# Border rows scaled whole and zeroed again, and TensorE's program written out, in a kernel of a deformable and a binarised convolution

## The reference, cut to what matters

```python
def _dcnv4(x, dw_w, dw_b, om_w, om_b, vp_w, vp_b, op_w):
    xdw = conv3x3_depthwise(x, dw_w, padding='SAME') + dw_b    # zero outside the image
    om = (xdw @ om_w + om_b).reshape(n, h, w, G, KK * 3)       # per group and tap: dx, dy, mask
    value = (x @ vp_w + vp_b).reshape(n, h, w, G, GC)
    # bilinear samples of value at (pixel + tap + offset), times mask, summed over the 9 taps
    return out @ op_w

x = x + _dcnv4(_gn(x), ...)
x = x + binarised_conv(_gn(x), ...)
```

## Time and profile before

| | us |
|---|---|
| median of 3 runs | 4247.4 (4243.7 to 4248.2) |
| the profiled execution | 4246.0 |
| its span, first to last instruction | 4244.2 |
| TensorE busy | 3872.8 (91%) |
| VectorE busy | 3561.1 (84%) |
| ScalarE busy | 2423.4 (57%) |
| GpSimd busy | 569.8 (13%) |
| mean granted TensorE clock | 0.973 |

### The profile page before, as it was taken

One profiled execution on the slowest core, in us unless ns is written; L12 is line 12 of the kernel. 1 busy time (PEld: TensorE's weight loads), 2 busy tenths in 40 slices (PEclk: granted clock), 3 DMA queues, 4 the chain that ended last, 5 costly groups with the idle time before them and its releaser, 6 DMA issues. The chain is left out here.

```text
span 4244.2 us, 94584 instructions
## 1 busy us (share of the span) xinstructions
PE 3872.8 (91%) x38382; PEld 2480.9 (58%) x38382; DVE 3561.1 (84%) x2896; ACT 2423.4 (57%) x5027; POOL 569.8 (13%) x480
## 2 busy tenths in 40 slices
PE   3899999999999999999999999999999985888988
PEld 1466666666666666666666666666666663333333
DVE  2799899989998899899989998999899993556554
ACT  4666666666666666666666666666666622333332
POOL 0011111111111111111111111111111110222222
PEclk9999999999999999999999999999999996999999
DMA  4454455445544554555445544554454433222321
GB/s 129 108 115 100 101 126 123 99 103 119 120 100 104 120 119 99 109 123 119 99 101 125 124 99 101 121 129 99 100 106 104 79 57 133 89 90 90 136 92 60
DMA packets 308092, 453.20 MB, mean 107 GB/s; under 512 B 33456, under 2 KB 239024, under 8 KB 301872
## 3 DMA queue, kind: packets, MB, share of 16 engines
q0 software_dynamic: 95168, 197.15, 25.9%
q1 hardware_dynamic: 212464, 249.71, 19.4%
HBM read 245.38 MB, written 67.11 MB: 74 GB/s over the span
## 5 line engine op out<-in xcount | busy, mean ns | idle before, releaser
L982 DVE TENSOR_TENSOR pv<-val,wsum 128x2048 f32<-128x2048 f32 x800 | 1810.3, 2283 | 11.1 <-PE ps_add L791 11.0
L791 PEld LDWEIGHTS ps_add<-ident,pv 128*128 128x128 f32 x12800 | 1399.7, 142 | 325.7 <-issue 220.7
L791 PE MATMUL ps_add<-ident,pv 128*128 128x128 f32 x12800 | 1525.0, 275 | 39.5 <-DVE pv L982 31.0
L746 PE MATMUL ps_om<-xdw,omw 128*32 128x256 f32 x13824 | 884.4, 389 | 124.7 <-ACT hat L579 109.1
L746 PEld LDWEIGHTS ps_om<-xdw,omw 128*32 128x32 f32 x13824 | 395.0, 111 | 431.7 <-ACT hat L579 120.8
L470 POOL DMA_DIRECT2D wsum<-prod x192 | 226.0, 1255 | 2688.6 <-DVE wsum L935 2688.6
L577 ACT ACTIVATE hat<-ps_om,omb 128x256 f32<-128x256 f32 x576 | 275.4, 478 | 537.0 <-PE ps_om L746 537.0
L935 DVE TENSOR_TENSOR prod<-hat,mwy 128x1536 f32<-128x1536 f32 (+1 forms) x384 | 525.2, 1395 | 59.0 <-DMA wsum<-prod 42.5
L1530 PE MATMUL ps_c<-c_sgn,c_ksgn 128*128 128x512 bf16 x2304 | 518.7, 384 | 2.5 <-DVE c_res L1647 2.5
L542 ACT ACTIVATE tri<-tri,gn_tri 96x512 f32<-96x512 f32 (+3 forms) x812 | 473.5, 647 | 6.0 <-DMA tri<-in_zeros_dram 0.5
L921 DVE TENSOR_TENSOR mwy<-hat,msk 128x768 f32<-128x768 f32 x288 | 274.1, 952 | 223.7 <-ACT hat L591 223.5
(11 more groups left out here) (102 smaller groups left out, 2791.2 us busy)
## 6 DMA issues: line engine op xcount, KB each, us to landing
wsum<-prod POOLq DMA_DIRECT2D x160, 768.0 KB, 6.9
tri<-in_x_dram SPq DMA_DIRECT2D x725, 128.0 KB, 2.9
win<-in_x_dram SPq DMA_DIRECT2D x144, 256.0 KB, 3.3
xres<-in_x_dram POOLq DMA_DIRECT2D x128, 256.0 KB, 9.0
x<-xres SPq DMA_DIRECT2D x128, 256.0 KB, 4.1
c_x<-x SPq DMA_DIRECT2D x8, 4096.0 KB, 13.0
out_dram<-c_x SPq DMA_DIRECT2D x32, 1024.0 KB, 4.0
acc<-in_x_dram POOLq DMA_DIRECT2D x14, 1024.0 KB, 5.6
```

The lines of the kernel that those rows point to most:

```text
L746: mm = nc.tensor.matmul(ps_om[G * q:G * q + G, (par + i) % 2, 0:TOK], omw[:, h, comp, :], xdw[:, j % 2, h, q, :], start=h == 0, stop=h == ...
L791: mm = nc.tensor.matmul(ps_add[:, tb, c, :], pv[:, (j + uv) % PBUF, c, P * tb:P * tb + P], consts["ident"][:, :], start=uv == 0 and c % 4 ...
L982: nc.vector.tensor_tensor(pv[:, (j + uv) % PBUF, :, :].rearrange("p c (r w) -> p c r w", w=W), val[:, :, SR * j + u:SR * j + u + SR, v:v + ...
```

## The change

Two edits. First, `normalise_tri` takes a tuple of `qp` and scales whole pieces; where both `qp` are normalised in one place, a piece covers both (96x1024). At an image's border the row outside is scaled along and then set to zero again by one `Copy` with scale 0, which waits on a new semaphore for the scaling to be done. `tri_normed` is raised by the number of `qp`, at the end. Second, TensorE's program of layer 0 calls `step` for all 32 steps with plain numbers, so its loop and its register arithmetic are gone. The other engines keep their loops.

```diff
-                def normalise_tri(n, j, h, qp):
-                    ...
-                    parts = [(0, KROWS, 2 * qp, 2 * qp + 2, 0, SR)]
-                    if j == 0 and qp == 0:
-                        parts = [(0, KROWS, 0, 1, 1, SR), (32, 64, 0, 1, 0, 1), (64, KROWS, 0, 1, 0, 1),
-                                 (0, KROWS, 1, 2, 0, SR)]
-                    elif j == STEPS - 1 and qp == 1:
-                        parts = [(0, KROWS, Q - 2, Q - 1, 0, SR), (0, KROWS, Q - 1, Q, 0, SR - 1),
-                                 (0, 64, Q - 1, Q, SR - 1, SR)]
+                def normalise_tri(n, j, h, qps):
+                    for qp in qps:
+                        ...
                     for c in range(CB):
-                        for p0, p1, q0, q1, r0, r1 in parts:
-                            v = tri_of(n, j, h)[p0:p1, c, q0:q1, r0:r1, :]
-                            last = nc.scalar.activation(v, v, ACT.Identity, bias=gn_tri[p0:p1, j % 2, 2 * c + 1, h:h + 1],
-                                                        scale=gn_tri[p0:p1, j % 2, 2 * c, h:h + 1])
-                    last.then_inc(tri_normed, 1)
+                        v = tri_of(n, j, h)[0:KROWS, c, 2 * qps[0]:2 * qps[-1] + 2, :, :]
+                        last = nc.scalar.activation(v, v, ACT.Identity, bias=gn_tri[0:KROWS, j % 2, 2 * c + 1, h:h + 1],
+                                                    scale=gn_tri[0:KROWS, j % 2, 2 * c, h:h + 1])
+                    outside = None
+                    if j == 0 and 0 in qps:
+                        outside = tri_of(n, j, h)[0:32, :, 0, 0, :]
+                    elif j == STEPS - 1 and 1 in qps:
+                        outside = tri_of(n, j, h)[64:KROWS, :, Q - 1, SR - 1, :]
+                    if outside is not None:
+                        last.then_inc(tri_scaled, 1)
+                        act.wait_ge(tri_scaled, 2 * CH * n + (0 if j == 0 else CH) + h + 1)
+                        last = nc.scalar.activation(outside, outside, ACT.Copy, scale=0.0)
+                    last.then_inc(tri_normed, len(qps))
...
-                for qp in range(2):
-                    normalise_tri(0, 0, 1, qp)
+                normalise_tri(0, 0, 1, (0, 1))
...
                         if k in DW_AT[1:3] and not last:
-                            normalise_tri(n1, j1, 1, DW_AT.index(k) - 1)
+                            normalise_tri(n1, j1, 1, (DW_AT.index(k) - 1,))
...
-                            for qp in range(2):
-                                normalise_tri(n2, j2, 0, qp)
+                            normalise_tri(n2, j2, 0, (0, 1))
...
-                steps_of_images(pe, step)
+                for n in range(NI):
+                    for j in range(STEPS):
+                        step(n, j, (n, j) == (0, 0), (n, j) == (NI - 1, STEPS - 1))
```

More of the change, by code:

```diff
@@ L284, in layer0 @@
         tri_loaded, tri_normed = [sem("tri_loaded0"), sem("tri_loaded1")], sem("tri_normed")
-        gn_spread = sem("gn_spread")
+        gn_spread, tri_scaled = sem("gn_spread"), sem("tri_scaled")
         bg_full, bg_free = sem("bg_full"), sem("bg_free")
@@ L524, in normalise @@
                     last.then_inc(win_normed, 1)
-                def normalise_tri(n, j, h, qp):
[L527 to L530, removed]
-                    parts = [(0, KROWS, 2 * qp, 2 * qp + 2, 0, SR)]
-                    if j == 0 and qp == 0:
-                        parts = [(0, KROWS, 0, 1, 1, SR), (32, 64, 0, 1, 0, 1), (64, KROWS, 0, 1, 0, 1),
-                                 (0, KROWS, 1, 2, 0, SR)]
-                    elif j == STEPS - 1 and qp == 1:
-                        parts = [(0, KROWS, Q - 2, Q - 1, 0, SR), (0, KROWS, Q - 1, Q, 0, SR - 1),
-                                 (0, 64, Q - 1, Q, SR - 1, SR)]
-                    for c in range(CB):
-                        for p0, p1, q0, q1, r0, r1 in parts:
-                            v = tri_of(n, j, h)[p0:p1, c, q0:q1, r0:r1, :]
-                            last = nc.scalar.activation(v, v, ACT.Identity, bias=gn_tri[p0:p1, j % 2, 2 * c + 1, h:h + 1],
-                                                        scale=gn_tri[p0:p1, j % 2, 2 * c, h:h + 1])
-                    last.then_inc(tri_normed, 1)
@@ new lines, in normalise_tri @@
+                def normalise_tri(n, j, h, qps):
+                    for qp in qps:
+                        if tri_of(n, j, h) is tri_first:
+                            act.wait_ge(tri_first_loaded[qp], 16 * tri_loads(j, qp))
+                        else:
+                            act.wait_ge(tri_loaded[qp], 16 * (tri_loads_before(n, j, h, qp) + tri_loads(j, qp)))
+                    for c in range(CB):
+                        v = tri_of(n, j, h)[0:KROWS, c, 2 * qps[0]:2 * qps[-1] + 2, :, :]
[11 more added lines that the diff above has]
+                    last.then_inc(tri_normed, len(qps))
@@ L626, in _ @@
                 act.wait_ge(val_zero, 6)
-                for qp in range(2):
-                    normalise_tri(0, 0, 0, qp)
+                normalise_tri(0, 0, 0, (0, 1))
                 act.wait_ge(weights_loaded, WL)
@@ L643, in _ @@
                 hats(0, 0, 1)
-                for qp in range(2):
-                    normalise_tri(0, 1, 0, qp)
+                normalise_tri(0, 1, 0, (0, 1))
                 def step(n, j, first, last):
```

## The result

| | before | after |
|---|---|---|
| median of the runs, us | 4246.3 (4243.7 to 4248.2, 4 runs) | 4146.5 (4144.0 to 4147.6, 4 runs) |
| span of the profiled execution | 4244.2 | 4143.6 |
| TensorE / VectorE busy | 3872.8 / 3561.1 | 3848.2 / 3560.1 |
| ScalarE busy | 2423.4 | 2288.7 |
| mean granted TensorE clock | 0.973 | 0.982 |

The ratio is 0.9765 (95% interval 0.9748 to 0.9782): 99.8 us less. The forecast was 4144 in a range of 4130 to 4180. Of all executions of this and the following kernels one, of d1_cut_in_j2_j3, was slow (5029.8 us at a granted clock of 0.746) and is left out of that kernel's median.

What follows compares the result with a forecast made beforehand. TensorE, held up by ScalarE's hats, was taken to bound j=0 and j=3, VectorE j=1 and j=2. Terms 66.5 + 2.8 + 4.3 + 6.9 + 22 = 102.5 us gave 4144 us, range 4130 to 4180 with the first two rivals.

Steps and rivals of the forecast that it cites:

- Start of j=3: Last step of seven images: shorter border-form scaling cuts TensorE's stalls for hats, 9.5 us an image, 66.5 us in all.
- the three parts: In j=3, per image: 5.3 us off the first stall, 2.3 from full clock behind it, 2.3 for the second stall.
- The 0.4 given away to VectorE: In j=3, 9.5 us an image was taken instead of 9.9, as VectorE is late next.
- Rival 1: VectorE takes over in j=3, so only 34 us come back instead of 66.5, giving 4176 us; chance 0.14.
- Before the loop: Start-up: the second border form's wait of 7.14 us shrinks by 5.3 and the matmuls behind it by 1.6, 6.9 us.
- j=0, plain form and closings: Starts of j=0: plain form's 0.62 us wait goes, 4.3 us; TensorE's loop removed at five closings, 22 us.
- Rival 2: Another engine's backward branch takes the place of TensorE's, so the 22 us do not come: 4166 us; chance 0.09.
- j=1 and j=2: Gain costed at zero in seven images, where VectorE is unbroken; 2.8 us taken in the last image.
- The pieces' own time: On ScalarE, the merged border form falls from 10.74 to 5.4 us, the unmerged one in j=3 from 7.91 to 3.4.
- rival 4: 96x1024 costs twice the 512 piece with no fixed part saved: 11 us less gain, 4155 us; chance 0.05.
- rival 3: TensorE's written-out program stalls for instruction fetch once in each step, 106 us, making it slower at 4271 us; chance 0.03.

Runs made afterwards that it cites:

- d1_cut_in_j2_j3: Changed kernel with the old cut pieces put back for steps j=2 and j=3 only: 4150.4 us, median of three runs.
- d2: Changed kernel with the old cut pieces put back for the second half of j=0, images after the first: 4162.0 us.
- f1: Changed kernel with VectorE's statistics reading 64 of every 512 columns, so its result is another one: 4090.7 us.
- e1: Changed kernel with TensorE's loop kept, so only the change to normalise_tri: 4161.4 us.
- e2: Kernel before with only TensorE's program written out, normalise_tri as before: 4230.5 us.
- e3: Changed kernel with pieces scaled whole but each qp for itself, eight of 96x512 instead of four of 96x1024: 4170.2 us.
- e5: Changed kernel with the loops of ScalarE, VectorE and SyncE written out too: 4145.2 us.
- h1: Changed kernel with SyncE's stores of a step's result moved behind the second twelve loads: 4138.2 us.
- after_again: The changed kernel itself, word for word, run again on the same chip as the two kernels with SyncE's order changed: 4147.2 us.
- h2: Changed kernel with SyncE's stores and second twelve loads both waiting for the first value unit of tap 4: 4162.5 us.

## Why the prediction was right

The forecast was 102.5 us of gain, the measurement 99.8. Step by step:

- *Start of j=3*, 66.5 predicted: j=3 is 69.6 us shorter in seven images, 9.9 an image, the full sum of the three parts. The 0.4 given away to VectorE was not needed, and the stall left is 1.25 and not 1.5. Rival 1 (VectorE takes over in j=3, 34 us) is refuted: VectorE idles 3.1 us for hats there still, d2 shows a wait of 2.30 costing 2.3, and f1 leaves j=3 unmoved.
- *Before the loop*, 6.9 predicted: the wait of 7.14 is 1.55, and the 48 matmuls take 5.30 for 6.88.

```profile
80.84 5.30 PE L717 MATMUL ps_bg<-pv,diag 128*32 128x512 f32 x48 [1.55 <-ACT xdw L552]
```

That is 5.6 + 1.6 = 7.2. The 3 us by which the first start comes earlier besides lie in the loads, which vary.
- *j=0, plain form and closings*, 4.3 + 22 = 26.3 predicted: 27.8. Here the price of the branch was right, 21.0 (e1) and 21.8 (e2). The plain form's 0.62 us went and come back in e3. Rival 2 (another engine's branch takes its place) is refuted by e5.
- *j=1 and j=2*, 2.8 predicted as gain in the last image and zero in the others: the last image gives 4.7 (j=1 100.0 to 99.6, j=2 103.9 to 99.6), but the seven others take 11.2 us more, so the two steps together are 6.5 longer. This is the step that failed: "I cost these at zero", and with it "22, all in the half that is TensorE's". I had taken the waits there for waits that only change their name. The waits themselves mostly did: in j=1 0.71 us for a hat and 1.34 for products became one wait of 2.13 for products, in j=2 2.93 for a hat became 2.69. What I left out is what stands behind the one wait. In five of the six images behind the first the clock fell after it, as it had after none of the two short ones, and these j=1 steps take 103.1 to 103.4 us where they took 101.5 to 101.9. In the sixth (the third image) the clock stayed and a further wait of 1.86 us came: 103.5. That is 9.7 of the 11.2; the first image's j=2 has the rest, with adds of 3.57 us after a wait of 2.60. That VectorE is what j=1 and j=2 wait for, f1 shows; that the lower clock is what made five of the steps longer is read from the traces (e1 and h1 have the same wait with full clock behind it at 101.5 to 102.0 us), and no run isolates it.

  It is tempting to say that VectorE had lived on the delay of the closings, and that it was this lead which went. The traces speak against it: before, the second image's j=1 follows a j=0 without a closing (103.5 us) and takes the same 101.5 us as the others, and e1 has the wait of 2.13 us in all six images though its closings are there. So the wait came with the pieces. Why e1, with the loop, had the clock fall in three images and the changed kernel in five stays open, and with it the 4 to 7 us that the loop's removal is worth less than the 21 to 22 in j=0. I had foreseen a rise of some 20 us in the waits for products; it was 37.6.
- *The pieces' own time*: 5.07 us busy for the merged form and its copy, 5.4 predicted; 3.3 for four pieces and a copy, 3.4 predicted. Merging is worth about 24 us in the medians (e3; 26 by the two ratios), where I had expected 12; rival 4 (no fixed part saved) is refuted.
- *Straight-line fetching* (rival 3): the "issue" waits left in layer 0 are in single matmuls of the group means, 0.5 us at most (1.4 in after_again), and where the profile names a releaser for them, in e1, it is VectorE's mean; written out for three more engines the time stays the same.

By terms: +3.1, +3.3 (start), +1.5, +1.9 (last image), -11.2 (the others), and -0.7 of the rest, which is within the spread of two executions. Together -2.1 against the profiled execution's forecast: a right total with one wrong term in it, covered by four small ones of the other sign.

The Trainium skill, "Runtime: NRT & Kernel Launch", "Instruction fetch mechanics", has a taken branch outside the fetched window stall for a fetch. e1 agrees at TensorE as far as a trace can show it, with 14.5 us of idle in five closings that nothing in the profile ends. It would hold for the three other engines as well; e5 finds no time in theirs, and at the closing at 913 us the changed kernel's trace has no "issue" wait of ScalarE or VectorE.

## What to carry to other kernels

A saving on one engine counts step by step: ask of each stretch which engine it ends for. Where the other engine is the bound, the wait moves, and that need not be free: two short waits of TensorE became one of 2.13 us here, the clock fell behind it in five images of six, and the step took 1.6 us more. So a term put at nothing because "the wait only changes its name" wants a look at the clock behind the new wait. Cutting an operation to spare a border cost more here than doing it whole and repairing the border: 20 pieces of 10.74 us against four and a small one of 5.07. And before moving work to a DMA, look at what its 7 us would be hidden behind.

## What was not expected of the hardware

- On ScalarE pieces of 96x1024 took 1233 ns, of 96x512 804 ns, and the copy of 32x256 414 ns:

```profile
L535 ACT ACTIVATE tri<-tri,gn_tri 96x512 f32<-96x512 f32 x248 | 181.2, 804 | 0.0
L535 ACT ACTIVATE tri<-tri,gn_tri 96x1024 f32<-96x1024 f32 x128 | 148.7, 1233 | 8.1 <-ACT gn_tri L506 4.5 <-DMA tri<-in_x_dram 3.5
...
L546 ACT ACTIVATE tri<-tri 32x256 f32<-32x256 f32 x31 | 12.8, 414 | 1.9
```

  Double the columns is half as much again. A partition count of 96 or 128 made no difference (1233 and 1235).
- What the granted clock did behind a stall did not go by the stall's length. In the changed kernel a wait of 2.13 us in j=1 was followed by 16 adds at 1.96 us (upper level, 2.4 GHz) in the third image and by 2.63 to 3.62 us in the five others; one of 2.69 us in j=2 by 1.96 to 1.97 us in four images and by 3.38 and 3.00 in two. Two stretches right behind a wait of 2.13 us, with the granted clock third from the end (0.52 is for the most part the lower level, 1.2 GHz):

```profile
614.50:618.00 3.50, 3.50 (x16) 3.17 (x16) 3.50 (x3) 0.15 (x1) 0.00 (x0) 0.52 1.11 191
1027.88:1029.77 1.89, 1.89 (x16) 1.73 (x16) 1.89 (x2) 0.15 (x1) 0.00 (x0) 1.00 1.11 192
```

  And one behind the wait of 2.69 us:

```profile
1133.10:1136.40 3.30, 3.28 (x16) 2.98 (x16) 3.30 (x3) 0.18 (x1) 0.00 (x0) 0.56 1.10 191
```

  In h2 a wait of 3.73 us was followed by full clock in the third image (1.97 us) and by the lower one in the second (3.68). In the kernel before all seven waits of 2.29 us in j=3 had full clock behind them, and of the seven of 2.85 to 2.93 us in j=2 of the first to seventh image three had it and four had not. So one row of a stall and what follows it tells little of the next image.
